# Attention with a mixture of experts on one core: where the normalisation, the router's logits, the first loads and the weight splits of an early attention step stand

## What is computed

```python
xn = layernorm(x)                                  # no weight, per token
# local attention: 8 heads of 32, blocks of 12 queries, each sees 24 keys (its block and the one before)
q = xn @ Wq.T * Q_SCALE * softplus(per_dim_scale); k = xn @ Wk.T * K_SCALE; v = xn @ Wv.T
logits = q.k + rel_shift(q . (pos @ Wrel.T)); logits = tanh(logits / 50) * 50
attn_out = softmax(logits) @ v @ Wpost.T
# mixture of experts: 8 experts of hidden size 704, 2 for each token
normed = rmsnorm(xn) * norm_weight
probs = softmax(normed @ router_weight.T); best two, weights renormalised
moe = xn + alpha * sum_e combine_e * (silu(gate_e) * up_e) @ down_e.T
out = x + attn_out + moe
```

## Time and profile before

| | |
|---|---|
| median of 3 runs | 876.99 us (870.02, 876.99, 895.14) |
| profiled execution: its own time, its span | 864.34 us, 862.5 us |
| TensorE busy, mean granted clock | 798.9 us (93%), 0.948 |
| DVE, ACT, POOL busy | 462.9, 342.5, 372.0 us |
| end of step 0, step 8, step 37 | 28.03, 121.95, 358.11 us |
| DMA | 110.75 MB, mean 128 GB/s |

### The profile page before, as it was taken

How to read it: one execution, slowest core, us unless ns; L and a number is a source line. 1 busy time by engine, 2 the same in 40 slices (tenths; PEclk the granted TensorE clock), 3 DMA queues, 4 the chain that set the end, 5 groups by cost and what they waited for, 6 DMA issues and landing times.

```text
span 862.5 us, 20398 instructions
## 1 busy us (share of the span) xinstructions
PE 798.9 (93%) x6883; PEld 771.7 (89%) x6883; DVE 462.9 (54%) x1085; ACT 342.5 (40%) x620; POOL 372.0 (43%) x273
## 2 busy tenths in 40 slices
PE   0899997899999999989999999999999999999993
PEld 0889997799899999888999999999999999999993
DVE  3623455789988544444444545554445445544452
ACT  4244564466554665523333333333333333333330
POOL 2133465577576676421344433333434333333422
PEclk9755998999999999969999999999999999999998
DMA  8734788679764442211236456255255363222221
GB/s 253 242 124 132 231 285 258 209 242 309 265 198 122 130 125 73 69 29 24 38 64 168 90 119 169 40 140 142 38 149 133 72 179 77 35 38 38 34 27 24
DMA packets 69253, 110.75 MB, mean 128 GB/s; under 512 B 15640, under 2 KB 52548, under 8 KB 69156
## 3 DMA queue, kind: packets, MB, share of 16 engines
q0 software_dynamic: 18304, 39.50, 19.5%
q1 hardware_dynamic: 37956, 47.87, 18.5%
q10 hardware_dynamic: 12896, 22.04, 8.0%
HBM read 66.66 MB, written 42.75 MB: 127 GB/s over the span
## 4 chain that ended last, share of the span: by engine, by line
PE 85%; DMA 4%; issue 4%; DVE 4%; ACT 1%; POOL 1%; ACTq 1%; SPq 0%; POOLq 0%; DVEq 0%
PE psum L1152 77%; PE psum L1245 4%; DMA bd_d<-arena 2%; PE psum L1210 1%; DMA arena<-bd_d 1%; DMA out<-spare,sca_i 1%; PE psum L1171 1%; PE psum L1315 1%; ACTq L692 1%; DVE xT L1036 1%; DVE arena L1105 1%; PE psum L1196 1%; PE psum L1324 1%; ACT xT L695 1%; DVE spare L849 0%
## 5 line engine op out<-in xcount | busy, mean ns | idle before, releaser
L1152 PE MATMUL psum<-w_ring,xT 128*128 x1608 | 278.4, 329 | 6.2 <-DVE xT L1036 4.1
L1152 PEld LDWEIGHTS psum<-w_ring,xT 128*128 128x128 f32 x1608 | 258.2, 189 | 19.6 <-issue 17.2
L600 POOL DMA_INDIRECT out<-spare,sca_i x67 | 106.6, 1591 | 276.1 <-DVE spare L1139 255.5
L1152 PE MATMUL psum<-w_ring,hT 128*128 x1139 | 151.5, 286 | 2.0 <-DVE spare L1139 1.4
L1025 DVE SCALAR_TENSOR_TENSOR spare<-psum,xg,spare 128x704 f32<-128x704 f32 x67 | 63.7, 950 | 166.6 <-PE psum L1152 166.6
L1152 PEld LDWEIGHTS psum<-w_ring,hT 128*128 128x128 f32 x1139 | 140.1, 190 | 2.4 <-issue 2.4
L785 ACT ACTIVATE spare<-psum,xg 128x704 f32<-128x704 f32 x67 | 56.8, 847 | 162.4 <-PE psum L1152 162.4
L591 POOL TENSOR_TENSOR arena<-arena,const 120x540 f32<-120x540 f32 x38 | 62.3, 1639 | 125.7 <-ACT arena L740 125.7
L695 ACT ACTIVATE xT<-psum,nwp 128x128 fp32r<-128x128 f32 x134 | 41.9, 364 | 159.6 <-PE psum L1210 143.2
L1152 PE MATMUL psum<-arena 32*120 32x108 f32 (+1 forms) x1216 | 91.9, 274 | 0.0
L1152 PEld LDWEIGHTS psum<-arena 32*120 32x120 f32 (+1 forms) x1216 | 86.9, 190 | 3.3 <-issue 0.2
(11 more groups left out here) (165 smaller groups left out, 986.3 us busy)
## 6 DMA issues: line engine op xcount, KB each, us to landing
w_split<-w_ring POOLq DMA_DIRECT2D x20, 1088.0 KB, 5.8
w_ring<-w_split SPq DMA_DIRECT2D x40, 544.0 KB, 3.8
raw<-in_w_raw ACTq DMA_DIRECT2D x32, 544.0 KB, 5.5
arena<-xn_d SPq DMA_DIRECT2D x34, 120.0 KB
arena<-in_x SPq DMA_DIRECT2D x37, 108.0 KB
out<-arena SPq DMA_DIRECT2D x37, 108.0 KB
bd_d<-arena SPq DMA_DIRECT2D x38, 84.4 KB
x_all<-in_x SPq DMA_DIRECT2D x3, 1024.0 KB, 9.6
```

Source lines behind the costliest of these rows:

```text
L600: pool.indirect_dma_start(out=out, out_offset=bass.IndirectOffsetOnAxis(ap=sca_i[:, b:b + 1], axis=0), in_=y[:, b % 2, :], in_offset=None, ...
L1152: return pe.matmul(out_ap, lhs, rhs, start=first, stop=last)
```

## The change

It moves work among the steps and engines; what is computed and the number of instructions of TensorE stay.

- SP: `const` (needed from step 3), the second 8 tiles of `x`, `wpost`, the router's weights and `alpha` are loaded after the five windows of the first groups, and `wv` ahead of `wq`.
- DVE ahead of the steps: the statistics come before the softplus of `per_dim_scale`, which now stands behind `rest_v(0)`; the relative-position weights are copied by 4 instructions, not 8; the router's weights are scaled in step 2.
- `vp_w` is split in two halves: `wv` ahead of the steps, `wpost` in steps 2 and 3.
- Statistics: 4, 4, 6, 6, 4 tiles at the end of steps 0 to 4. Tiles 8 to 31 are normalised by POOL, 4 a step, in steps 2, 3 and 5 to 8, and POOL starts their stores.
- Logits: steps 4 to 11 in place of 1 to 8, and so the routing from step 12 (`S_R`) in place of 9.
- Pieces of the experts' weights: loaded from step 5, rounded and split in steps 8 to 39 in place of 3 to 34.
- `store_scale`: end of step 33 in place of 9.

```diff
-        S_R = TT // TPS + 1
+        S_L = 4
+        S_R = S_L + TT // TPS
...
+        S_D = {2: 1, 3: 4}
...
         def logit_tiles(s):
-            return range(TPS * (s - 1), TPS * s) if 1 <= s and TPS * s <= TT else range(0)
+            return range(TPS * (s - S_L), TPS * (s - S_L + 1)) if 0 <= s - S_L < TT // TPS else range(0)
+        def stat_tiles(s):
+            return range(*((8, 12), (12, 16), (16, 22), (22, 28), (28, 32))[s]) if s < 5 else range(0)
         def late_tiles(s):
-            return range(XCH, 2 * XCH) if s == 1 else range(2 * XCH + 4 * (s - 3), 2 * XCH + 4 * (s - 2)) if 3 <= s <= 6 else ()
+            first = XND + 4 * (s - S_D[2] - 1) if s <= S_D[2] + 2 else 2 * XCH + 4 * (s - S_D[3] - 1)
+            return range(first, first + 4) if S_D[2] < s <= S_D[2] + 2 or S_D[3] < s <= S_D[3] + 4 else range(0)
         def pieces(s):
-            n = s - 3
+            n = s - 8
+            return range(n, n + 1) if 0 <= n < NSPL else range(0)
+        def raw_loads(s):
+            n = s - 5
             return range(n, n + 1) if 0 <= n < NSPL else range(0)
...
-            sp.dma_start(const[:, :], const_d[:, 0:NC]).then_inc(s_const, 16)
             load_part(1)
+            sp.dma_start(vp_raw[:, WV, :, :], wv.rearrange("(k p) e -> p k e", p=P)).then_inc(s_wv, 16)
...
-            load_part(2)
...
+            load_part(2)
+            sp.dma_start(const[:, :], const_d[:, 0:NC]).then_inc(s_const, 16)
+            sp.dma_start(vp_raw[:, WP, :, :], wpost.rearrange("(k p) e -> p k e", p=P)).then_inc(s_wp, 16)
...
+            def layernorm(t):
+                pool.tensor_scalar(xn_all[:, t, :], x_all[:, t, :], mean[:, t:t + 1], small[:, 2, t:t + 1],
+                                   ALU.subtract, ALU.mult).then_inc(s_xnd, 1)
...
+                if s == S_D[2] + 1:
+                    pool.wait_ge(s_nb, 3)
+                if s == S_D[3] + 1:
+                    pool.wait_ge(s_nb, 4)
+                for t in late_tiles(s):
+                    layernorm(t)
+                    for i in range(2, len(PARTS)):
+                        if t == PARTS[i][1] - 1:
+                            store_xn(i)
+                if s == 3:
+                    rest_vp(WP)
                 for n in pieces(s):
                     split(n)
...
-                if s == 1:
-                    deviation(2)
-                if s == 3:
-                    deviation(3)
-                    act.wait_ge(s_st, len(CHUNKS) + 1)
-                    act.activation(small[:, 3, :], small[:, 4, :], ACT.Sqrt).then_inc(s_sq, 1)
...
+                if s == S_D[3] + 1:
+                    deviation(3)
+                for n in raw_loads(s):
+                    load_raw(n)
...
+                if s == 2:
+                    round_vp(WP, s_wp)
+                if s == S_D[2]:
+                    deviation(2)
+                if s == S_D[3] + 1:
+                    act.wait_ge(s_st, len(CHUNKS) + 1)
+                    act.activation(small[:, 3, :], small[:, 4, :], ACT.Sqrt).then_inc(s_sq, 1)
+                if s == NG - 5:
                     store_scale()
...
-                if s in (1, 2):
-                    tile_stats(XCH * (s + 1), XCH * (s + 2))
-                for t in late_tiles(s):
-                    layernorm(t)
+                if s == S_D[2] + 1:
+                    spread_of(2)
+                if s == S_D[3] + 2:
+                    token_scale()
...
-                if s == 0:
-                    tile_stats(XCH, 2 * XCH)
-                    spread_of(2)
+                if stat_tiles(s):
+                    tile_stats(stat_tiles(s)[0], stat_tiles(s)[-1] + 1)
+                for i in (2, 3):
+                    if s == S_D[i]:
+                        variance_of(i)
```

More of the change, by code:

```diff
@@ L221, in program @@
         mv = sb("mv", [P, TT, 2])
+        mean, var = mv[:, :, 0], mv[:, :, 1]
         st6 = spare[:, 13, 0:TT * 6].rearrange("p (t n) -> p t n", n=6)
@@ L868, in token_scale @@
                 dve.tensor_scalar(small[:, 4, :], small[:, 5, :], RMS_EPS, None, ALU.add).then_inc(s_st, 1)
+            def token_scale():
                 dve.wait_ge(s_sq, len(CHUNKS) + 1)
                 dve.reciprocal(s_tok[:, :], small[:, 3, :]).then_inc(s_stok, 1)
-            for i in range(2):
-                tile_stats(*CHUNKS[i])
-                spread_of(i)
-            def layernorm(t):
-                dve.tensor_scalar(xn_all[:, t, :], x_all[:, t, :], mean[:, t:t + 1], small[:, 2, t:t + 1],
-                                  ALU.subtract, ALU.mult).then_inc(s_xnd, 1)
@@ L879, in _ @@
[L879 to L887 removed]
+            tile_stats(*CHUNKS[0])
@@ new lines, in _ @@
+            variance_of(0)
+            dve.wait_ge(s_ea, 1)
+            dve.tensor_scalar(q_scale[:, 4:5], q_scale[:, 3:4], 1.0, None, ALU.add).then_inc(s_qs, 1)
+            spread_of(0)
+            tile_stats(*CHUNKS[1])
+            variance_of(1)
+            spread_of(1)
+            dve.wait_ge(s_rel, 1)
+            for i in range(HC):
+                rows = slice(DH * i, DH * (i + 1))
+                dve.tensor_copy(rel_bd[rows, :, i, :], psum[rows, 3, 0:KD * NPOS].rearrange("p (k n) -> p k n", k=KD)).then_inc(
+                    s_qs, 1)
```

112 lines of the change are left out of this document (55 added, 57 removed).

## The result

The kernel after takes 840.70 us (median of 4 executions, 839.65 to 845.56) against 875.15 us of the kernel before (4 executions, 870.02 to 895.14): a ratio of 0.9636, 95% interval 0.9569 to 0.9703. A second measurement (run 9) gave 841.95 against 870.64 us, 0.9703 (0.9656 to 0.975). The profiled execution took 839.92 us, its span is 838.1 us, 24.4 us less than before. The gain is thus 34 us by these medians, 29 by those of the second measurement and 24.4 by the profiles; the profiled execution of the kernel before was shorter than its four timed ones. Ratios leave out executions that took over 1.5% more than the shortest of the same kernel.

The account below looks back on a forecast made before the run. TensorE was taken to bound the kernel, by its waits and half clock. 20.8 + 7.3 - 0.1 = 28.0 us gave 836.3 us from the profile, 849.0 from the median; forecast 846 us, range 832 to 866.

Parts of the forecast that it names:

- Ahead of the steps: Before the steps: first normalisation at 10.8 us, first `rows_v` at 18.1; step 0 ends 3.7 us earlier, at 24.3.
- Step 1: Second step, now without logits, the clock risen or rising in it: 4.8 us, bounds 3.5 and 6.1.
- Step 2: TensorE idles some 4 us for biases read back behind `add_x(0)`; clock falls again; ends at 40.5 us, bounds 36 and 43.
- Step 3 and the clock: Clock back in step 3, 8.0 us; then steps with logits at full clock, 8.8 us and seven of 9.29.
- The term of 20.8 us: Three steps of 7.03 us won, less 0.3: step 11 ends at 122.3 us, where step 8 ended at 121.95.
- `store_scale`: Store of `s_tok` moved from step 9 to 33: 7.3 us won; 0 to 7.3 may return at step 35.
- GpSimd's normalisation: Steps 2, 3 and 5 to 8: 0.7 us a tile, 2.8 us a step, hidden; the bound only above 1.7 a tile.
- Splits in the last steps: Splits five steps later, also in steps 35 to 39: 0 to 1 us lost in the last steps, taken as 0.1.
- The offset: Profiled execution lies 12.7 us below the median of 876.99: 836.3 us from the profile, 849.0 from the median.
- the rule weighed: Throttled clock is the default and activity releases it; over 50 us busy at half clock disagreed, so the slower case stayed.
- the slower rival: Logits at half clock throughout steps 4 to 11: 6.4 us more a step, all eight give 900 us; chance 0.04.
- My account of why the clock rose at 89 us: Kernel before, step 5: the clock rose in the first step in which the output projection runs.

Follow-up runs that it names:

- run 9: The kernel after, unchanged, timed again as a control: 841.95 us against 870.64 us for the kernel before.
- run 4: Kernel after with the loads of tiles 16 to 31 (2 MB) behind the first two group rows of `x` for `add_x`: 846.99 us, ratio 0.9727.
- run 5: Kernel after with the loads of tiles 16 to 31 behind the return of the first biases: 841.3 us, ratio 0.9651.
- run 7: Kernel after with tiles 8 to 31 normalised by VectorE in place of GpSimd: 848.71 us, ratio 0.9745.
- run 3: Kernel after with the store of `s_tok` in step 12 in place of 33: 851.86 us, ratio 0.98.
- run 1: Kernel before with the store of `s_tok` at the end of step 33 in place of 9: median 887.34 us.
- run 10: Kernel after with two pieces of experts' weights in each of steps 9 and 10, so that the pieces end in step 37: 854.85 us, ratio 0.9866.
- run 6: Kernel after with the logits in steps 2 to 9 in place of 4 to 11: 871.06 us, ratio 0.9901.
- run 12: Kernel after, loads of tiles 16 to 31 behind the first biases' return and `s_tok` stored in eight parts, steps 26 to 33: median 842.1, ratio 0.9611.
- run 2: Kernel before with only the logits moved, to steps 4 to 11 from 1 to 8, routing with them: 859.69 us, ratio 0.9848.

## Why the prediction was right, and where not

The forecast was 846 us, range 832 to 866, 0.74 for faster; it was 840.70, and the mechanism was the one forecast: steps 1 to 3 without logits let the clock come back, and the steps with logits then ran at it. By its steps, against the profiled execution:

- **Ahead of the steps**: step 0 ended at 24.45 (forecast 24.3). Right, with the first normalisation at 10.59 (10.8) and `rows_v` at 18.36 (18.1).
- **Step 1**: 3.78 us (4.8). Its matmuls have the durations of the full clock from its first on, so that my lower bound of 3.5 was the nearer one.
- **Step 2**: the place of the wait was right, its size was not: 10.10 us in place of 4, and the step 16.5 in place of 11.4 us. The term that I mis-sized is the landing of `x`: I took 29 us because "the new order of loads has as much in front of it in this queue". It was 33.5 us. And I put no price on the biases' own write, which was started behind 2 MB of `x`: with the rows for `add_x` there by 27.2 us (run 4), this write alone held the read back, 8.8 us from its issue where 2.6 would do (run 5).
- **Step 3 and the clock**: the clock was back in step 3 (6.24 us, forecast 8.0), and steps 4 to 11 took 125.83 - 50.98 = 74.85 us, where I had 8.8 + 65.0 = 73.8. The excess of 1.1 us is steps 5 and 9; in step 9 ScalarE's next load waits 1.46 us for GpSimd's split of its buffer (in run 7, with less on GpSimd, the step takes 9.30).
- **The term of 20.8 us** came out as 17.5: 0.1 - 1.0 + 5.1 - 1.8 + 1.1 = 3.5 us later at the end of step 11, of which step 2 alone is more than all, and the plain step of 7.13, not 7.03, gives 0.3 back. That the sum missed by 3.3 us and not by 5.1 is luck: steps 1 and 3 were shorter than I had them.
- **`store_scale`**: forecast 7.3. The stall of step 11 is gone in full (run 3 gives 7.6 us back), but the routing's long steps were some 3 us longer, which I had priced at nothing ("Steps 12 on have the same work for all engines as before from step 9 on"). Whether the later splits cause that isn't shown: run 1, with the splits of the kernel before, has 13.31 and 14.26 us in steps 13 and 20, where the first profile has 12.12 and 10.07. A return at step 35 of 0.3 to 5.0 us occurs in other executions (0.7 in run 9, the kernel after itself), inside my 0 to 7.3.
- **GpSimd's normalisation**: 1.25 us a tile, not 0.7; hidden all the same. Taking the addition as nearest was wrong by a factor of 1.8; what saved the step is that I had worked out the point from which it decides.
- **Splits in the last steps**: 0.1 us forecast. They can hit VectorE's mask (2.84 in place of 0.48 us), but without them that part was no shorter (run 10).
- **The offset**: 836.3 from the profile and 849.0 from the median; the result lies between. The profiled execution of the kernel after took 839.92 us, 3.6 more than the sum gives from the profile, and the other medians of the kernel before are 869.8 to 870.8 us, so that the median of 876.99 was a high one. That 846 came so near rests on this choice between two bases as much as on the sum.

**What the rule weighed is worth.** The rows now show TensorE busy for 76, 90 and more us at 0.50 (runs 1, 6 and 12). The Trainium skill (TensorE: Matmul & The Clock Gate, Part 1: The HAM clock gate) says that activity releases the throttled state; here it did so late or not at all while the logits ran, and within a step or two where there were none. I was right to keep the slower rival alive, and its mechanism exists, but I tied it to the kernel after, where none of eight executions shows it. It is one wait in a logits step away, as runs 10 and 12 show, and runs 5 and 7 have one execution each of about 900 us whose granted clock (0.90) looks the same, so eight executions don't rule it out.

My account of why the clock rose at 89 us (the first projection) was incomplete: in runs 1 and 12 the rise, too, came behind the projection of a step with logits, but in steps 8 and 11, after three and six steps whose projections had not ended it; in run 2 it came in step 2, which has neither, and in run 6 with the queries and keys of step 10, the first without logits. In a step with logits the scores, `rows_v` and the projection ahead of that place are the longest piece without a router's product, so it may be that piece which lets the clock rise; what holds it down otherwise (the 8-column products, the transposes, their order) wasn't taken apart. Shown is that in steps without logits it rose within the step or at the start of the next (runs 2, 5, 6 and 12, and the kernel after) and that moving the logits two steps up (run 6) brings the half clock back.

## What to carry to other kernels

When a stretch runs at the half clock though the engine is busy, look at which work fills it: moving one kind of work (here the router's logits) away from the place where the clock falls bought 10 us by the median (run 2), and 17.5 by the profile together with the edits that keep TensorE from waiting there; moving it two steps back lost 15 us at the least and 30 by the median. Then read each queue in order for what stands ahead of the first small transfer that somebody waits for: 2 MB of loads not yet needed made the 2.6 us of a small write 8.8 us. And judge a local gain by several executions: a version that was 7 to 8 us ahead after the first steps was no faster by its median, and in the long one that was profiled the half clock that followed a wait of 1.13 us cost it some 50 us.

## What the runs showed of the hardware

- TensorE fully busy can stay at 1.2 GHz (0.50) for over 110 us: run 12, from 50 to about 166 us. A step with logits then takes 16.97 us in place of 9.30.
- In steps with logits the clock fell behind idle stretches of 0.84 us (run 2), 1.13 us (run 12) and 2.50 us (run 10), and stayed down for some 14, 116 and 17 us. The length of the idle stretch alone doesn't tell: in step 3, without logits, 1.46 us were followed by no fall in the kernel after and by 3.4 us at the half clock in run 5, and 2.06 us by no fall in run 12.
- In step 0, before and after, `rows_v` takes 1.60 to 1.61 us as in stretches at 0.50 (0.95 at 1.00), and queries and keys 3.74 in place of 2.0 us, while the windows give 1.00. At the start of the program the granted clock in the records doesn't tell the matmuls' real speed; their durations do.
- VectorE's multiplication of 120x324, 0.48 us alone, takes 2.4 to 2.8 us when GpSimd's split (2.49 us) starts with it, and 3.92 us (run 12) beside three operations of GpSimd that follow each other, the split of `wpost`, `add_x` and its own mask: about as long as GpSimd's work lasts.
- GpSimd's tensor_scalar with two per-partition scalars, 128x256: 1.21 to 1.31 us (VectorE, in the kernel before: 0.42).
- A store of 4096 pieces of 4 bytes held up the transfers behind it by 7.2 to 7.6 us beside the stores of pieces (step 11 before, step 14 in run 3), and in step 33 by 0 to 0.7 us in seven profiles and 5.0 in one; in eight stores of 512 pieces it costs nothing that a step shows.
